# Gathered rows in two permanent buffers, an early signal for one strip, one output tile, and new prologue and epilogue orders, in a residual-chain kernel on one core

## The chip, the core and the metric

The kernel runs on one core of a Trainium2 chip. The core has four computing engines that run their own instruction streams: TensorE (PE in the profile, PEld for its weight loads), VectorE (DVE), ScalarE (ACT) and GpSimd (POOL). SyncE (SP) issues most of the transfers; 16 DMA engines carry them. Streams meet only at semaphores. The metric is the device time of one execution in microseconds (us), as the median of the runs.

## The reference, cut to what matters

A tensor x of 128 entries, 64 rows each, 256 features, passes through four residual layers. Each layer takes its weights or gains from a condition vector of the entry or from class ids of the row:

```python
x = x + einsum('bsd,bde->bse', x, weight(U, V)) + bias     # L0: U = mu @ W_dec + b_dec, rank 30
x = x + clip((x * style) @ weight.T * dcoef + bias)          # L1: modulated product
x = x + (relu(x @ w_down) @ w_up + x)                        # L2: w_down, w_up scaled per entry (dg, ug, ub)
h = ln(ln(x, pw_g[pathway], pw_b[pathway]), cp_g[c], cp_b[c])
t = ln(x, tm_g[c], tm_b[c]);  s = ln(x, ms_g[m], ms_b[m])
cat = concat(w0*h, w1*t, w2*(x+mem), w3*(x+noi), w4*(x+res), w5*s)
x = x + ln(silu(cat @ W1 + b1) @ W2 + b2, g, be)             # L3
```

`pw_g[pathway]` and `pw_b[pathway]` are 512 numbers for each of the 8192 rows, out of a table with 250 rows.

## The kernel before, in words

The 8192 rows are cut into 16 chunks of 512 rows (8 entries). About 70 stages, each a small function of one chunk, carry a chunk through the four layers. A stage is called with its engine and a chunk, waits for its semaphores, and issues its instructions. The order in which an engine runs the stages is written out by hand in three lists for `run_slots`: `begin` (the setup, mixed with the first chunks), `order` (one iteration of the steady loop; a stage with lag 3 works on the chunk three behind the iteration's number; ten iterations, numbers 6 to 15) and `end` (the last chunks). An engine runs its list strictly in order, so a stage that waits holds all stages behind it.

The setup decodes U for all entries (16 groups: `act_turn`/`v_turn`, `pe_dec`, `v_decode`), and makes the per-entry tables: `style` and `dcoef` for L1, `dgdb` and `ugub_scratch` for L2, and the row that L3 adds for each entry (`pe_mo`, `v_mostat`, `g_moroot`, `v_monorm`, `pe_mot`, `pe_row`, `v_rows`, `act_rowwrite`), besides the split weights of L3 (`act_w1scale`, `v_w1sum`, `act_w1high`, `g_w1tlow` and others).

The stages that the argument follows, for a chunk c, in the order of the data:

- `act_u`, `pe_t`, `act_th1`, `act_th2`, `g_tlow`, `pe_x1`, `v_x1add`: layer 0. `pe_t` makes 30 rows t. `act_th1` brings them to SBUF (`t_f`), `act_th2` copies them rounded into three strips of `t_st`, and `g_tlow` overwrites the first strip with what the rounding lost. Each of the two ACT stages adds one to the semaphore `a_th`.
- `g_style`, `pe_l1`, `v_l1mul`, `v_l1min`, `v_x2add`: layer 1.
- `pe_dn`, `v_dnmul`, `v_dnadd`, `act_relu`, `g_wup` (two POOL operations on the tile `ugub`, which `load_up` has filled), `pe_up`, `v_x3sum`: layer 2.
- `pe_x3r`, `v_xstat`, `g_rootx`, `act_x3`, `act_xnorm`, `pe_xht`: the first norm of layer 3 (`xhat`).
- `g_gather`: four indirect DMAs, issued by POOL, that fetch the 512 gathered table rows into `pw_rows`. `g_hmul` multiplies `xhat` with their first half and `g_hadd` adds the second; `v_hstat`, `g_rooth`, `act_hnorm`, `v_hprod`, `pe_hht` follow.
- `pe_w1_x3`, `pe_w1_tm`, `pe_w1_ms`, `pe_w1_h`, `act_silu`, `v_sillow`, `pe_w2`, `act_ysquare`, `g_rooty`, `v_ygain`, `v_ynorm`, `store`: the two products of layer 3 and the output.
- `pe_warm` issues matmuls on a tile of ones, with no use of their result; the table `WARM` says which semaphore each group waits for and how many there are.

There is one `pw_rows`, so `g_gather(c)` waits for `g_hadd(c-1)`. There are two output tiles `y_out`; `v_ynorm(c)` waits until the store of chunk c-2 has landed. All SP transfers, loads and stores, stand in one order: in an iteration ids, shift, x, ub, up, and the store last.

## Time and profile before

| | |
|---|---|
| median of 3 runs | 519.87 us (519.48 to 520.92) |
| the profiled execution, its own time | 522.03 us |
| its span, first to last instruction | 520.2 us |
| PE busy in the span | 486.5 us (94%), 3216 matmuls |
| DVE / ACT / POOL busy | 411.8 / 356.9 / 406.3 us |
| moved by DMA | 61.82 MB |

A span of one engine's busy time near the length of a stretch says that this engine sets the pace there; where it is shorter, the timeline says after each gap in brackets what the engine waited for. The granted clock (PEclk) is a share of TensorE's full 2.4 GHz: 1.00 is 2.4 GHz and 0.50 is 1.2 GHz.

### The profile page before, as it was taken

What the parts mean: (1) busy time and instruction counts of PE and PEld (TensorE: products, weight loads), DVE (VectorE), ACT (ScalarE), POOL (GpSimd) and SP (SyncE); (2) the same over time, 40 slices, a digit from 0 to 9 for tenths busy, and PEclk for the clock granted to TensorE, in tenths of its full rate; (3) what the DMA queues carried; (4) which work ended last, traced back from release to release, by engine and by line L of the source; (5) the groups of instructions that cost most, each with busy time, mean ns of one, the idle gap of its engine ahead of it and who ended that gap; (6) DMA issues with size and microseconds to landing.
All of it is one profiled execution on the core that took longest, in us unless ns stands there. A gap on an engine that the chain in (4) does not pass through costs nothing.

```text
span 520.2 us, 9616 instructions
## 1 busy us (share of the span) xinstructions
PE 486.5 (94%) x3216; PEld 360.9 (69%) x3245; DVE 411.8 (79%) x701; ACT 356.9 (69%) x667; POOL 406.3 (78%) x380
## 2 busy tenths in 40 slices
...
DMA packets 35118, 61.82 MB, mean 119 GB/s; under 512 B 5108, under 2 KB 17542, under 8 KB 34709
## 3 DMA queue, kind: packets, MB, share of 16 engines
...
## 4 chain that ended last, share of the span: by engine, by line
PE 74%; ACT 8%; DVE 7%; issue 5%; POOL 4%; DMA 1%; DVEq 0%; ACTq 0%; POOLq 0%
PE ps_d L966 10%; PE ps_c L916 9%; PE ps_c L918 9%; PE ps_c L917 9%; PE ps_d L980 5%; PE ps_a L994 4%; PE ps_b L916 3%; PE ps_b L917 3%; PE ps_b L918 3%; PE ps_b L1012 3%; PE ps_a L1006 2%; POOL pw_rows L1532 2%; PE ps_a L1012 2%; DMA set_wdec<-in_W_dec 1%; PE ps_b L935 1%
## 5 line engine op out<-in xcount | busy, mean ns | idle before, releaser
L1232 ACT ACTIVATE h<-h,nb_h,rstd_h 128x256 f32<-128x256 f32 x64 | 33.3, 591 | 41.1 <-POOL nb_h L1562 41.1
L966 PE MATMUL ps_d<-xm_t,l_w 128*128 128x512 f32 x128 | 59.6, 609 | 1.6 <-DVE h L1455 0.9
L1532 POOL DMA_INDIRECT pw_rows<-in_pw,gidx x40 | 39.0, 976 | 12.2 <-issue 12.2
L1577 POOL TENSOR_TENSOR h<-xhat,pw_rows 128x1024 f32<-128x1024 f32 x16 | 38.0, 2372 | 6.4 <-ACT xhat L1232 6.4
L966 PEld LDWEIGHTS ps_d<-xm_t,l_w 128*128 128x128 f32 x128 | 23.5, 193 | 26.6 <-issue 24.5
L1598 POOL TENSOR_TENSOR w_up<-w_up,ugub 128x1024 f32<-128x1024 f32 x16 | 39.0, 2436 | 1.3
L1582 POOL TENSOR_TENSOR h<-h,pw_rows 128x1024 f32<-128x1024 f32 x16 | 38.3, 2394 | 1.2
L1596 POOL TENSOR_TENSOR w_up<-up_rep,ugub 128x1024 f32<-128x1024 f32 x16 | 38.1, 2379 | 1.1 <-issue 0.9
L1608 POOL TENSOR_TENSOR x3be<-x,ln_gb 128x1024 f32<-128x1024 f32 x16 | 37.9, 2371 | 0.6 <-DVE y_out L1513 0.6
L916 PE MATMUL ps_b<-w_h,act_t_l 128*128 128x256 f32 x128 | 37.7, 294 | 0.4 <-DVE act_t_l L1477 0.4
L994 PE MATMUL ps_a<-act_dn,w_up 128*128 128x128 f32 x256 | 32.5, 281 | 5.9 <-ACT act_dn L1211 5.3
L994 PEld LDWEIGHTS ps_a<-act_dn,w_up 128*128 128x128 f32 x256 | 31.1, 195 | 9.0 <-issue 7.2
L1343 ACT ACTIVATE y_sq<-ps_b 128x256 bf16<-128x256 f32 x64 | 23.6, 378 | 18.9 <-PE ps_b L918 18.9
L1232 ACT ACTIVATE xhat<-ps_a,nb_x,rstd_x 128x256 f32<-128x256 f32 x64 | 30.9, 563 | 7.9 <-POOL nb_x L1562 7.9
L917 PE MATMUL ps_b<-w_l,act_t_h 128*128 128x256 f32 x128 | 36.1, 282 | 0.0
L918 PE MATMUL ps_b<-w_h,act_t_h 128*128 128x256 f32 x128 | 36.0, 281 | 0.0
L1455 DVE TENSOR_TENSOR h<-ps_d,h 128x1024 f32<-128x1024 f32 x16 | 19.6, 1224 | 18.0 <-ACT h L1232 15.0
L1445 DVE TENSOR_TENSOR ps_d<-ps_d,xh_t 128x1024 f32<-128x1024 f32 x16 | 19.7, 1229 | 17.5 <-PE ps_d L1049 17.5
L1263 ACT ACTIVATE tm_t_h<-ps_a 128x1024 fp32r<-128x1024 f32 x16 | 16.4, 1025 | 25.0 <-DVE ps_a L1440 25.0
L1379 DVE TENSOR_TENSOR ps_d<-ps_d,dcoef 128x1024 f32<-128x1024 f32 x16 | 19.7, 1232 | 15.0 <-PE ps_d L966 13.7
L1532 POOL DMA_INDIRECT pw_rows<-in_pw,pw_idx x24 | 24.1, 1003 | 9.1 <-issue 6.5
L1200 ACT ACTIVATE t_st<-idx_t 30x512 fp32r<-30x512 f32 x48 | 30.0, 625 | 0.5
...
## 6 DMA issues: line engine op xcount, KB each, us to landing
...
pw_rows<-in_pw,gidx POOLq DMA_INDIRECT x40
```

Source lines behind the costliest of these rows:

```text
L916: eng.matmul(out, wl, ah, start=first, stop=False)
L917: eng.matmul(out, wh, al, start=False, stop=False)
L918: return eng.matmul(out, wh, ah, start=False, stop=last)
L966: m = eng.matmul(ps_l1[:, o, :], l1_w[:, k, o * P:(o + 1) * P], xm_t[:, k, :], start=k == 0, stop=k == KB - 1)
L994: m = eng.matmul(ps_up[:, k, j * P:(j + 1) * P], w_up[:, j, k * P:(k + 1) * P], act_dn[:, j, :, :], start=True, stop=True)
L1232: m = eng.activation(out[:, j, :], src[:, j, :], ACT.Identity, bias=nb[k][:, j:j + 1], scale=rstd[k][:, j:j + 1])
L1532: eng.indirect_dma_start(pw_rows[:, j, :], None, t["pw"], bass.IndirectOffsetOnAxis(ap=idx[:, j:j + 1], axis=0)).then_inc(s_pw[c.ring], 16)
L1577: eng.tensor_tensor(h1[:, :, :], xhat[:, :, :], pw_rows[:, :, 0:D], ALU.mult).then_inc(g_h1m, 1)
L1582: eng.tensor_tensor(h1[:, :, :], h1[:, :, :], pw_rows[:, :, D:2 * D], ALU.add).then_inc(g_h1, 1)
L1596: eng.tensor_tensor(w_up[:, :, :], q, ugub[:, :, 0:D], ALU.mult).then_inc(g_upm, 1)
L1598: eng.tensor_tensor(w_up[:, :, :], w_up[:, :, :], ugub[:, :, D:2 * D], ALU.add).then_inc(g_up, 1)
L1608: eng.tensor_tensor(x3be[c.ring][:, :, :], x3[:, :, :], ln_be[:, :].unsqueeze(1).broadcast_to([P, CT, D]), ALU.add).then_inc(g_x3be, 1)
```

## The change

Six edits go together.

1. `pw_rows` becomes two tiles, one for even and one for odd chunks. `g_gather(c)` waits for `g_hadd(c-2)`. Gathers 0 and 1 stand one behind the other near the top of POOL's `begin`, while the decoder runs.
2. `act_th2` signals after its first strip, so `a_th` counts three for a chunk, and `g_tlow` waits for the first strip only. All other waits on `a_th` are renumbered to the same events.
3. To make room, several setup tiles move into tiles that are idle during the setup (`wsq` and `style2` in `w_up`, `dm` and `st_nr` in `x3_t`, `ugub_row` in `dn_v` and `dn`), with waits where the tile is first used (`v_x1add(1)`, `v_dnmul(0)`, `v_x3low(0)`).
4. One `y_out` instead of two: `v_ynorm(c)` waits for the store of chunk c-1. The last two chunks write into `xm_t` and `x1_even` and wait for no store. In SP's loop the store moves ahead of `load_up` and serves the chunk one later (lag 5 for 6).
5. `act_u(0)` is split in two halves, the first of which waits for 8 of the 16 decoder groups.
6. New `begin` and `end` orders on all five engines, and other counts in `WARM`. The loop orders of PE, ACT, DVE and POOL are unchanged.

```diff
-        pw_rows = sb("pw_rows", [P, CT, 2 * D])
+        pw_rows = [sb(f"pw_rows{r}", [P, CT, 2 * D]) for r in range(2)]
...
-        y_out = [late(f"y_out{r}", [P, CT, D]) for r in range(2)]
+        y_out = late("y_out", [P, CT, D])
...
+        y_late = {NCH - 2: rows_in(xm_t), NCH - 1: rows_in(x1_even)}
...
-        WARM = ((z_pool, 1, ps_b, 0, 24), (c_ug, 1, ps_d, 0, 17), (v_dca, 1, ps_a, 0, 8), (v_row, 1, ps_c, 0, 5),
-                (v_cls, 1, ps_c, 1, 2), (v_row, 1, ps_c, 0, 15), (v_ub, 1, ps_b, 1, 6))
+        WARM = ((z_pool, 1, ps_b, 0, 24), (c_ug, 1, ps_d, 0, 11), (v_dca, 1, ps_a, 0, 11), (v_row, 1, ps_c, 0, 8),
+                (v_cls, 1, ps_c, 1, 3), (v_row, 1, ps_c, 0, 3), (v_ub, 1, ps_b, 1, 8))
...
 def act_u
+            if first(c):
+                eng.wait_ge(v_dec, NG // KB)
+                eng.activation(u_ch[0][:, 0], src[:, 0], ACT.Copy)
+                eng.wait_ge(v_dec, NG)
+                eng.activation(u_ch[0][:, 1], src[:, 1], ACT.Copy).then_inc(a_u, 1)
+                return
...
 def act_th2
-            for lo in (0, RP, 2 * RP):
+            eng.activation(t_st[0:RK, :], t_f, ACT.Copy).then_inc(a_th, 1)
+            for lo in (RP, 2 * RP):
...
 def v_ynorm
-            wait(eng, s_store[c.ring], 16 * c.half)
+            if isinstance(c.n, int) and c.n in y_late:
+                wait(eng, p_l1, NCH)
+                wait(eng, v_x3t, NCH - 1)
+            else:
+                wait(eng, s_store[1 - c.ring], 16 * (c.half + c.ring))
...
 def g_gather
-            wait(eng, g_h1, c.n)
+            wait(eng, g_h1, c.n - 1)
+            wait(eng, s_pw[c.ring], 16 * CT * c.half)
...
 def g_tlow
-            wait(eng, a_th, 2 * c.n + 2)
+            wait(eng, a_th, 3 * c.n + 2)
...
 SP
-                      order=[(load_ids, 2), (load_shift, 3), (load_x, 0), (load_ub, 0), (load_up, 0), (store, 6)],
+                      order=[(load_ids, 2), (load_shift, 3), (load_x, 0), (load_ub, 0), (store, 5), (load_up, 0)],
...
 PE begin, from the last decoder group on
-                             (pe_dec, 14), (pe_dec, 15), (pe_ug, 0), (pe_warm, 6), (pe_t, 0), (pe_warm, 1),
-                             (pe_x1, 0), (pe_dc, 0), (pe_t, 1), (pe_hid, 0), (pe_l1, 0), (pe_mo, 0), (pe_x1, 1),
-                             (pe_dn, 0), (pe_t, 2), (pe_warm, 2), (pe_up, 0), (pe_x3r, 0), (pe_l1, 1),
-                             (pe_x1, 2), (pe_mot, 0), (pe_xht, 0), (pe_cls, 0), (pe_dn, 1), (pe_row, 0),
-                             (pe_t, 3), (pe_cp, 0), (pe_up, 1), (pe_warm, 3), (pe_warm, 4), (pe_x3r, 1),
-                             (pe_hht, 0), (pe_l1, 2), (pe_warm, 5), (pe_shift, 0), (pe_tm, 0), (pe_dn, 2),
-                             (pe_w1_x3, 0), (pe_ms, 0)],
+                             (pe_dec, 14), (pe_dec, 15), (pe_ug, 0), (pe_warm, 6), (pe_dc, 0), (pe_t, 0),
+                             (pe_warm, 1), (pe_x1, 0), (pe_hid, 0), (pe_t, 1), (pe_l1, 0), (pe_x1, 1),
+                             (pe_mo, 0), (pe_dn, 0), (pe_warm, 2), (pe_t, 2), (pe_up, 0), (pe_mot, 0),
+                             (pe_x3r, 0), (pe_l1, 1), (pe_x1, 2), (pe_cls, 0), (pe_xht, 0), (pe_dn, 1),
+                             (pe_row, 0), (pe_t, 3), (pe_up, 1), (pe_cp, 0), (pe_warm, 3), (pe_x3r, 1),
+                             (pe_warm, 4), (pe_warm, 5), (pe_l1, 2), (pe_shift, 0), (pe_hht, 0), (pe_w1_x3, 0),
+                             (pe_tm, 0), (pe_dn, 2), (pe_ms, 0)],
...
 DVE begin, behind the first chunk's x1
-                             (v_w2centre, 0), (v_dcrcp, 0), (v_softmax, 0), (v_l1mul, 0), (v_l1min, 0),
-                             (v_x2add, 0), (v_x1add, 1), (v_w1sum, 0), (v_dnmul, 0), (v_dnadd, 0),
-                             (v_mostat, 0), (v_x3sum, 0), (v_xstat, 0), (v_monorm, 0), (v_l1mul, 1),
+                             (v_softmax, 0), (v_dcrcp, 0), (v_w2centre, 0), (v_l1mul, 0), (v_l1min, 0),
+                             (v_x2add, 0), (v_mostat, 0), (v_x1add, 1), (v_dnmul, 0), (v_dnadd, 0),
+                             (v_monorm, 0), (v_x3sum, 0), (v_w1sum, 0), (v_xstat, 0), (v_l1mul, 1),
...
 POOL begin
-                      begin=[(g_ones, 0), (g_init, 0), (g_gather, 0), (g_b2rows, 0), (g_tlow, 0), (g_style, 0),
-                             (g_dcoef, 0), (g_tlow, 1), (g_wup, 0), (g_style, 1), (g_moroot, 0), (g_w1tlow, 0),
-                             (g_tlow, 2), (g_w1xlow, 0), (g_rootx, 0), (g_w2low, 0), (g_w1mlow, 0), (g_hmul, 0),
-                             (g_hadd, 0), (g_wup, 1), (g_rooth, 0), (g_style, 2), (g_gather, 1), (g_res, 0),
-                             (g_rootx, 1), (g_wup, 2), (g_hmul, 1), (g_tlow, 3), (g_hadd, 1), (g_gather, 2),
-                             (g_rooth, 1), (g_style, 3), (g_res, 1), (g_rootx, 2)],
+                      begin=[(g_ones, 0), (g_init, 0), (g_gather, 0), (g_gather, 1), (g_b2rows, 0), (g_tlow, 0),
+                             (g_style, 0), (g_dcoef, 0), (g_tlow, 1), (g_wup, 0), (g_moroot, 0), (g_style, 1),
+                             (g_tlow, 2), (g_rootx, 0), (g_w1tlow, 0), (g_hmul, 0), (g_hadd, 0), (g_wup, 1),
+                             (g_rooth, 0), (g_style, 2), (g_w1xlow, 0), (g_res, 0), (g_rootx, 1), (g_w1mlow, 0),
+                             (g_w2low, 0), (g_wup, 2), (g_hmul, 1), (g_tlow, 3), (g_hadd, 1), (g_res, 1),
+                             (g_rooth, 1), (g_style, 3), (g_gather, 2), (g_rootx, 2)],
...
 POOL end, its first two chunks
-                      end=[(g_wup, 13), (g_hmul, 12), (g_hadd, 12), (g_tlow, 14), (g_rooty, 10), (g_gather, 13),
-                           (g_rooth, 12), (g_res, 12), (g_style, 14), (g_rootx, 13), (g_wup, 14), (g_hmul, 13),
+                      end=[(g_wup, 13), (g_gather, 13), (g_hmul, 12), (g_rooty, 10), (g_hadd, 12), (g_tlow, 14),
+                           (g_res, 12), (g_rooth, 12), (g_style, 14), (g_wup, 14), (g_rootx, 13), (g_hmul, 13),
...
 ACT end, its first stages
-                      end=[(act_hnorm, 12), (act_u, 15), (act_silu, 11), (act_silh, 11), (act_th1, 15),
+                      end=[(act_u, 15), (act_hnorm, 12), (act_silu, 11), (act_th1, 15), (act_silh, 11),
```

## Rows read from the trace of the kernel before

**Rows 1.** The page: its first line and the busy time of TensorE.

```profile
span 520.2 us, 9616 instructions
PE 486.5 (94%) x3216; PEld 360.9 (69%) x3245; DVE 411.8 (79%) x701; ACT 356.9 (69%) x667; POOL 406.3 (78%) x380
```

**Rows 2.** Windows, PE alone: stretch, busy and matmuls, granted clock, DMA share.

```profile
core 0: us, PE busy (x), PEclk, DMA share, GB/s
50.00:100.00 50.00, 40.41 (x263) 0.93 0.36 97
100.00:400.00 300.00, 297.83 (x2024) 1.00 0.41 111
...
455.00:510.00 55.00, 50.42 (x282) 1.00 0.19 58
```

**Rows 3.** Windows again, for the DMA engines and the clock in the setup.

```profile
24.00:46.00 22.00, 18.09 (x146) 1.00 1.01 290
46.00:52.00 6.00, 5.04 (x62) 1.00 0.04 15
...
57.40:64.00 6.60, 5.19 (x20) 0.50 0.29 87
```

**Rows 4.** Timeline of PE, setup: start, length, what, idle time before.

```profile
50.48 1.90 PE L542 MATMUL ps_a<-ones 128*128 128x512 bf16 x8
56.27 2.85 PE L994 MATMUL ps_a<-act_dn,w_up 128*128 128x128 f32 x16 [3.89 <-ACT act_dn L1211]
60.53 1.94 PE L1006 MATMUL ps_a<-ident,x_t 128*128 128x128 f32 x8 [1.41 <-DVE x_t L1419]
...
100.22 1.04 PE L1012 MATMUL ps_a<-ident,xhat 128*128 128x128 f32 x8
```

**Rows 5.** Timeline of POOL, setup.

```profile
22.64 0.95 POOL L1532 DMA_INDIRECT pw_rows<-in_pw,pw_idx  x1 [0.30 <-issue]
...
46.40 2.38 POOL L1596 TENSOR_TENSOR w_up<-up_rep,ugub 128x1024 f32<-128x1024 f32 x1
...
57.63 0.20 POOL L833 TENSOR_SCALAR set_mo_ve<-set_mo_mv 128x3 f32<-128x3 f32 x1 [4.11 <-DVE set_mo_mv L644]
...
83.53 1.12 POOL L1532 DMA_INDIRECT pw_rows<-in_pw,pw_idx  x1 [0.16 <-issue]
...
88.45 2.37 POOL L1608 TENSOR_TENSOR x3be<-x,ln_gb 128x1024 f32<-128x1024 f32 x1
```

**Rows 6.** Timeline of DVE, setup.

```profile
48.86 2.90 DVE L685 TENSOR_TENSOR set_w1x<-set_wdec 128x512 f32<-128x512 f32 x1 [0.39 <-ACT set_wdec L772]
51.80 2.27 DVE L686 TENSOR_TENSOR set_w1x<-set_w1x,set_wdec 128x512 f32<-128x512 f32 x1
...
59.16 1.22 DVE L1419 SCALAR_TENSOR_TENSOR x_t<-x_even,ps_a 128x1024 f32<-128x1024 f32 x1 [1.62 <-PE ps_a L994]
...
64.08 0.38 DVE L1430 BATCH_NORM_AGGREGATE mv_x<-bn_x 128x2 f32<-128x6 f32 x4
...
66.84 0.96 DVE L655 TENSOR_TENSOR set_mo<-ps_c,set_wdec 128x768 f32<-128x768 f32 x1
```

**Rows 7.** DMA queues from 83.5 to 92: packets, MB, share of 16 engines.

```profile
q0 software_dynamic: 320, 1.05, 36.2%
```

**Rows 8.** Timeline of PE, epilogue.

```profile
413.82 0.65 PE L935 MATMUL ps_b<-x_t,u_ch 128*30 128x64 f32 x32 [0.87 <-ACT u_ch L1181]
...
463.66 0.50 PE L916 MATMUL ps_c<-ms_t_h,w_l 128*128 128x512 f32 x1 [0.92 <-DVE ms_t_l L1464]
...
474.59 0.39 PE L1092 MATMUL ps_c<-onehot,shift 128*128 128x512 bf16 x1 [0.87 <-DVE act_t_l L1483]
...
491.08 0.39 PE L1026 MATMUL ps_a<-onehot,gain_tab 24*128 24x512 bf16 x2 [1.08 <-ACT xh_t L1253]
```

**Rows 9.** Timelines of DVE and SP around an output, end of the loop.

```profile
406.22 1.66 DVE L1513 SCALAR_TENSOR_TENSOR y_out<-ps_b,rstd_y,x3be 128x256 f32<-128x256 f32 x4
...
435.44 1.66 DVE L1513 SCALAR_TENSOR_TENSOR y_out<-ps_b,rstd_y,x3be 128x256 f32<-128x256 f32 x4
```

More of the change, by code:

```diff
@@ L402, in split_in_place, with y_tile @@
             link(eng.tensor_copy(p3, src))
+        def y_tile(c):
+            return y_late[c.n] if isinstance(c.n, int) and c.n in y_late else y_out
         v_link = chain(nc.vector, v_chain)
@@ L1368, in v_x1add @@
             if isinstance(c.n, int) and c.n == 1:
-                eng.wait_ge(m_dc, 1)
+                eng.wait_ge(m_tail, 1)
                 eng.wait_ge(m_st, 1)
                 eng.wait_ge(m_ug, 1)
+                eng.wait_ge(m_hid, 1)
+                eng.wait_ge(d_ub, 48)
+                eng.wait_ge(v_pick, 1)
             eng.tensor_tensor(x1_t[c.ring][:, :, :], ps_x1[:, :, :], x_t[c.ring][:, :, :], ALU.add).then_inc(v_x1, 1)
@@ L1466, in low @@
             return stage
-        v_x3low = low(x3_t_l, x3_t, x3_t_h, a_x3h, v_x3l, (m_tail, 1), (m_st, 1), (m_ug, 1), (m_hid, 1), (d_ub, 48))
+        v_x3low = low(x3_t_l, x3_t, x3_t_h, a_x3h, v_x3l, (v_mo, 2))
         v_tmlow = low(tm_t_l, ps_tm, tm_t_h, a_tmh, v_tml, (m_row, 1), (d_row, 16))
@@ L1692, in _ @@
-                             (act_th1, 4), (act_x3, 2), (act_xnorm, 2), (act_hh, 1), (act_th2, 4), (act_tmh, 1),
-                             (act_x3h, 2), (act_relu, 3), (act_ysquare, 0), (act_msh, 1), (act_xht, 2),
-                             (act_gidx, 3), (act_onehot, 2)],
+                             (act_turn, 13), (act_turn, 15), (act_dg, 0), (act_vhigh, 0), (act_style, 0),
+                             (act_ug, 0), (act_exp, 0), (act_u, 0), (act_u, 1), (act_th1, 0), (act_th2, 0),
+                             (act_sqrt, 0), (act_u, 2), (act_hid, 0), (act_th1, 1), (act_th2, 1),
@@ L1734, in _ @@
                            (v_l1min, 13), (v_x2add, 13), (v_hlow, 11), (v_tmprod, 11), (v_dnmul, 13),
-                           (v_dnadd, 13), (v_tmlow, 11), (v_msprod, 11), (v_hstat, 12), (v_mslow, 11),
-                           (v_ygain, 10), (v_ynorm, 10), (v_x3low, 12), (v_x1add, 14), (v_x3sum, 13),
+                           (v_dnadd, 13), (v_tmlow, 11), (v_msprod, 11), (v_ygain, 10), (v_mslow, 11),
+                           (v_ynorm, 10), (v_hstat, 12), (v_x3low, 12), (v_x1add, 14), (v_x3sum, 13),
@@ L1737, in _ @@
                            (v_hprod, 12), (v_xstat, 13), (v_sillow, 11), (v_l1mul, 14), (v_l1min, 14),
                            (v_x2add, 14), (v_hlow, 12), (v_tmprod, 12), (v_dnmul, 14), (v_dnadd, 14),
-                           (v_tmlow, 12), (v_msprod, 12), (v_hstat, 13), (v_mslow, 12), (v_ygain, 11),
-                           (v_x3low, 13), (v_ynorm, 11), (v_x3sum, 14), (v_x1add, 15), (v_hprod, 13),
+                           (v_tmlow, 12), (v_hstat, 13), (v_msprod, 12), (v_ygain, 11), (v_x3low, 13),
@@ L1741, in _ @@
+                           (v_mslow, 12), (v_ynorm, 11), (v_x3sum, 14), (v_hprod, 13), (v_x1add, 15),
                            (v_xstat, 14), (v_sillow, 12), (v_l1mul, 15), (v_l1min, 15), (v_x2add, 15),
-                           (v_hlow, 13), (v_tmprod, 13), (v_dnmul, 15), (v_tmlow, 13), (v_dnadd, 15),
-                           (v_x3low, 14), (v_msprod, 13), (v_hstat, 14), (v_ygain, 12), (v_mslow, 13),
-                           (v_x3sum, 15), (v_ynorm, 12), (v_hprod, 14), (v_sil0, 13), (v_xstat, 15),
@@ L1745, in _ @@
-                           (v_msprod, 14), (v_sil1, 13), (v_hlow, 14), (v_tmprod, 14), (v_mslow, 14),
-                           (v_tmlow, 14), (v_hstat, 15), (v_ygain, 13), (v_x3low, 15), (v_ynorm, 13),
-                           (v_sil0, 14), (v_sil1, 14), (v_tmprod, 15), (v_hprod, 15), (v_tmlow, 15),
-                           (v_msprod, 15), (v_hlow, 15), (v_mslow, 15), (v_ygain, 14), (v_ynorm, 14),
+                           (v_hlow, 13), (v_tmprod, 13), (v_x3low, 14), (v_dnmul, 15), (v_dnadd, 15),
```

136 lines of the change are left out of this document (73 added, 63 removed).

## The prediction

> **What bounds the kernel now.** I began with the page's totals: TensorE is busy 94% of the span [rows 1]. The windows of PE say where the rest is [rows 2]. From 100 to 400 us it is busy 297.83 of 300, so in the loop nothing but PE's own work counts. Two stretches are loose: 50 to 100 (40.41 of 50, and part of that is `pe_warm`) and 455 to 510 (50.42 of 55, 4.6 idle). The change leaves PE's useful instructions and all loop orders but SP's alone, so it can act only through how early the loop starts and how tightly the epilogue packs. Next I read PE's timeline for what ends its gaps, then the engines named there, and last the DMA windows.
>
> In the setup PE runs eight warm matmuls at 50.48, then waits 3.89 us for `act_relu(0)` and starts `pe_up(0)` at 56.27; `pe_x3r(0)` waits 1.41 more [rows 4]. DVE shows why: between `v_x1add(1)` and `v_dnmul(0)` stands `v_w1sum`, 2.90 and 2.27 us [rows 6], where an operation with twice the elements takes 1.22 in the same rows. During it POOL is in `g_wup(0)`, from 46.40 [rows 5]. Behind the gap the granted clock is 0.50, the 1.2 GHz level, from 57.4 to 64 [rows 3]; eight transposes that take 1.04 at full clock (at 100.22) took 1.94 there [rows 4]. The loop's first `pe_xht` is at 100.22 [rows 4], my mark for the end of the setup.
>
> The second fact is the DMA engines: share 1.01 from 24 to 46, then 0.04 [rows 3]. Until 46 us they are full, and what comes last out of that backlog is `ugub` for chunk 0. `g_wup(0)` starts at 46.40 [rows 5], which is when the backlog ends.
>
> **The change part by part, setup.** The sum is made against the profiled execution (span 520.2, own time 522.03). The median of the runs is 519.87, so 2.2 us come off at the end.
>
> *Gather 1 moved.* Its POOL time is 83.53 to 88.45, 4.9 us [rows 5]. There it sits in front of `g_res(0)`, `g_rootx(1)`, `g_wup(2)` and `g_hmul(1)`, thus of the path to the loop. Behind gather 0 (last piece at 22.64, [rows 5]) it takes 4.9 us of a stretch in which POOL has little to do: `g_b2rows` slips by 4.9, and `g_tlow(0)`, with ACT now running `act_exp` and `act_u(1)` first, by about 1.5. What that delays is `pe_x1(0)`; `pe_dc`, the exponential and a `u` that used to lie behind it now lie ahead, so I find `v_x2add(0)` within 0.3 us of before. Of the 4.9 saved, `g_w1xlow`, `g_w1mlow` and `g_w2low`, which move behind, take 3.8 back (three operations of 512 columns; half of the 2.37 of 1024 in [rows 5] plus overhead, 1.25 each). Net gain: 1.1.
>
> *Gather 1 as traffic.* A gather took 36.2% of 8.5 us of all 16 engines, 3.1 us [rows 7]. At 24 to 29 us it is put in front of a full backlog, so that ends at 49.4, not 46.3, if nothing overlaps; 46.3 if the gather hides wholly. From DMA: Bandwidth & Descriptors, in the Trainium skill, section on SWDGE, HWDGE and iDMA: each engine goes round-robin over its queues. Hence GpSimd's queue would get its share at once, at the cost of SP's. With that page's 436 GB/s the estimate would be 2.4 us of delay instead of 3.1.
>
> *The new order in front of `pe_up(0)`.* `v_w1sum` moves behind `v_x3sum(0)`, `v_mostat` in front of `v_dnmul(0)`. Now `v_dnmul`, `v_dnadd` and `v_mostat` fill the 3.6 us from the end of `v_w1sum` at 54.07 [rows 6] to `g_moroot` at 57.63 [rows 5]; I give `v_mostat`, the longest, 2.4. The dn path ends at 56.3 - 5.1 + 2.4 = 53.6. The other leg is `g_wup(0)`: 4.8 us from the landing. Landing at 49.4 ends it at 54.2, and `g_moroot` (1.1) follows at 55.3. `v_monorm` now precedes `v_x3sum(0)` and waits for it; it takes 3.4 (64.4 to 67.8, [rows 6]). So `v_x3sum(0)` starts at 58.7 against 59.16, `v_w1sum` with POOL idle costs 1.3 (twice half of 1.22), `v_xstat(0)` 2.0, and mv_x is ready at 63.3, against 64.46 [rows 6]: 1.2 earlier. With the landing hidden, `g_wup(0)` starts as soon as POOL is free, by my walk at 44.3, and ends at 49; `v_monorm` then waits for `v_dnadd(0)` only, starts at 52.8, and mv_x is ready at 60.8: 3.7 earlier. Where between? The 0.50 clock may return, since PE still has two gaps of some 2 us here; that costs 0.9 on `pe_x3r(0)`, the difference in [rows 4]. I take the DMA delay as full, for the rows say full, and the clock as half likely.
>
> The setup then gives 1.2 + 1.1 = 2.3, up to 4.8 with the landing hidden, 1.4 with the slow clock. The row write of the setup gains a little because gather 1 no longer runs beside it. I take 2.5.
>
> *Early strip, `act_u` halves.* `act_th2` is three equal copies, so `g_tlow` may start two copies (1.3 us) earlier. In the loop PE never waits for it. In the setup it is inside the sum above. At nothing beyond that; if POOL were late it could give 1.3 once.
>
> *Moved tiles and their waits.* All are long past when asked: `v_x1add(1)` waits for `m_hid`, `d_ub`, `v_pick`, some 10 us old. Zero. If `m_hid` were late, `v_x1add(1)`, `v_mostat`'s successors and all of chunk 0's dn would queue behind it.
>
> **Loop.** `v_ynorm` comes at 406.22 and 435.44, one period apart, 27 to 29 us [rows 9]. The store now issues right behind it, since SP's waits in front of it (shift, x, ub) end earlier in the iteration; half a megabyte takes a few us at the 111 GB/s mean of [rows 2] (4.7). So the one tile has over 20 us of slack. `load_up` now stands behind the store, and what is queued behind it are the next ids, shift and x; but its own wait for `g_wup` ends later in the iteration than `v_ynorm` does. Zero. Bound: a late store would cost its lateness in each of ten iterations.
>
> **Epilogue.** Idle that names a cause: 0.87 for `u_ch(15)`, 0.92 for `ms_t_l`, 0.87 for `act_t_l`, 1.08 for `xh_t` [rows 8], and 4.6 in all from 455 to 510 [rows 2]. `act_u(15)` goes first on ACT, which removes the first. But gather 13 goes in front of `g_hmul(12)`: `g_hadd(12)` is 6 us later, `g_tlow(14)` too, and `pe_x1(14)` moves ahead of `pe_up(13)`. I walked these chunks: PE waits 0.4 for `ms_t_l(11)`, 0.5 for `g_tlow(14)` and 0.5 for `xhat(13)`. Net -0.5. In the next iteration `g_res(13)`, `g_style(15)` and gather 14 come out ahead, +0.6. In the last two, PE waits at most 1 us in five places where it waited 4.1. Sum: -0.5 + 0.6 + 3.1 = 3.2; my walk has no semaphore latency, so 2.7. Bounds 0.5 and 4. The tail behind the last product keeps its stages.
>
> **Sum.** 2.5 + 0 + 2.7 = 5.2. Span 515.0, profiled 516.8, median 514.7.
>
> **Rivals.**
> A. *Gather 1 hides in the backlog.* For it: the share counts overlap (1.01 is not a hard wall). Against: nothing idle from 24 to 46. Setup 4.8, sum 7.5: 512.4. Chance 0.17.
> B. *The backlog and the clock eat the setup's gain.* `ugub(0)` lands at 50 and PE stays at 0.50 for 7 us again. Setup about 0, epilogue 2.7: 517.2. Chance 0.20.
> C. *Nothing: the loop's start takes it back.* PE's idle in the loop is 2.2 of 300 [rows 2], so an earlier start can hardly be lost there; the epilogue would have to be pure shuffling, held by POOL and DVE. 519.5. Chance 0.07.
> D. *Slower: `ugub(0)` decides.* From the landing on the path is one for one: `g_wup`, `g_moroot`, `v_monorm`, `v_x3sum`. A landing at 49.4 leaves the setup 2.3 ahead, one at 51.7 nothing, and from 54.4 on (51.7 and the epilogue's 2.7) the kernel is slower. For it, `g_wup(0)` already starts as the backlog ends, and broadcast loads and the gather share engines. Against, that takes 8 us of delay where [rows 7] show 3.1. At 56: setup -4.3, epilogue 2.7, 521.5. Chance 0.06.
> A side risk within all: `v_w1sum` shows that a DVE operation with two SBUF operands waits while POOL computes, 2.90 for 0.6 of work [rows 5, 6]. `v_x3low(14)` now meets `g_wup(15)`: up to 1.6, inside my epilogue bound. (SBUF — State Buffer, section "SBUF: two separate sides", in the Trainium skill calls it an exclusive lock held for a whole instruction; the trace agrees.)
>
> **How the numbers follow.** Forecast 0.50, A 0.17, B 0.20, C 0.07, D 0.06. A measurement here tells 0.3% (1.6 us) from no change. Forecast and A are faster; of B, three in twenty fall within 0.3%; C is same, D slower: faster 0.84, same 0.10, slower 0.06. Eight in ten: from 511.4 (A with a full epilogue) to 518.4 (B with an epilogue of 1.5). The forecast's own range is 513 to 516.5.
>
> **What would show it.** PE's first loop `pe_xht` near 97.7 (A: 95.4; B: 100; D: past 103). POOL's `w_up` start near 49.4 with idle in front of it. DMA share near 1 until 49. No 0.50 clock, or a shorter one. `v_w1sum` at 1.3 us. PE idle from 455 on down from 4.6 to about 1.5, with new small gaps near 400 to 420 from `g_tlow(14)`. `v_ynorm` never waiting for a store. A loop period that differs, or idle there, would make me wrong at the root.

## The result and the profile after

Six runs of the changed kernel gave a median of 524.00 us (521.74 to 525.21); the kernel before had 521.24 beside it. The ratio is 1.0057, 95% interval 1.0036 to 1.0078: slower by 0.6%, where I had forecast 514.7 and a range up to 518.4. Measured again with a later group (`c0_after` below) the same kernel had 531.76 against 522.25, ratio 1.0153 (1.0108 to 1.0198). So the loss is real and not always of one size.

The page's first lines, and the windows of PE that answer to [rows 1, 2]:

```profile
span 523.4 us, 9602 instructions
PE 485.3 (93%) x3207; PEld 361.2 (69%) x3236; DVE 417.8 (80%) x701; ACT 355.9 (68%) x667; POOL 406.7 (78%) x380
```

```profile
50.00:100.00 50.00, 40.71 (x279) 0.97 0.35 84
100.00:400.00 300.00, 294.78 (x1990) 0.99 0.43 112
455.00:510.00 55.00, 51.29 (x290) 1.00 0.13 39
```

PE is busy for as long as before; the span is 3.2 longer. The middle row is the surprise: 294.78 in the stretch where [rows 2] had 297.83, so 3 us of new idle time lie in the loop, which no loop order of PE, ACT, DVE or POOL explains. DVE is busy 6 us longer with the same 701 instructions: something made them last longer.

PE's timeline, the rows that answer to [rows 4, 8]:

```profile
54.45 2.02 PE L1001 MATMUL ps_a<-act_dn,w_up 128*128 128x128 f32 x16 [0.93 <-ACT act_dn L1223]
59.46 1.06 PE L1013 MATMUL ps_a<-ident,x_t 128*128 128x128 f32 x8 [0.28 <-DVE x_t L1435]
98.02 1.06 PE L1019 MATMUL ps_a<-ident,xhat 128*128 128x128 f32 x8 [0.57 <-DVE tm_t_l L1480]
106.46 0.80 PE L923 MATMUL ps_c<-ms_t_h,w_l 128*128 128x512 f32 x1 [2.82 <-DVE ms_t_l L1480]
130.14 1.10 PE L1019 MATMUL ps_a<-ident,xhat 128*128 128x128 f32 x8
...
403.11 1.04 PE L1019 MATMUL ps_a<-ident,xhat 128*128 128x128 f32 x8
410.93 0.71 PE L960 MATMUL ps_b<-t_st,v_st 96*128 96x512 f32 x2 [0.87 <-POOL t_st L1569]
419.25 3.67 PE L973 MATMUL ps_d<-xm_t,l_w 128*128 128x512 f32 x8 [0.94 <-DVE h L1471]
432.87 1.04 PE L1019 MATMUL ps_a<-ident,xhat 128*128 128x128 f32 x8
```

The setup did what was forecast in this trace: the first loop `pe_xht` is at 98.02 (97.7 forecast, 100.22 before). Then the first iteration, number 6, takes 32.12 us to the next mark, where the kernel before took 27.44. The lead of 2.2 becomes a lag of 2.5 there, and it stays: just behind the loop the mark is 403.11 against 400.66.

DVE and POOL around that gap (both timelines of the changed kernel; the second number is the length):

```profile
98.82 6.46 DVE L1480 TENSOR_TENSOR x_t_l<-x_t,x_t_h 128x1024 fp32r<-128x1024 f32 x1
105.20 1.21 DVE L1480 TENSOR_TENSOR ms_t_l<-ps_d,ms_t_h 128x1024 fp32r<-128x1024 f32 x1
```

```profile
98.25 1.28 POOL L1569 TENSOR_TENSOR t_st<-idx_t,t_st 30x512 fp32r<-30x512 f32 x1 [0.47 <-ACT t_st L1210]
99.50 2.39 POOL L1603 TENSOR_TENSOR h<-h,pw_rows 128x1024 f32<-128x1024 f32 x1
101.85 2.34 POOL L1629 TENSOR_TENSOR x3be<-x,ln_gb 128x1024 f32<-128x1024 f32 x1
108.40 0.20 POOL L1575 TENSOR_TENSOR nm_h<-mv_h,mone 128x4 f32<-128x4 f32 x1 [4.21 <-DVE mv_h L1446]
```

This is nearly all of iteration 6's loss of 4.7 us. `v_x3low(1)` subtracts one SBUF tile from another; alone it takes 1.22. It starts at 98.82, while POOL computes, and ends at 105.28, 1.1 us after POOL's third operation in a row ends (104.19). `v_mslow(0)`, now behind it in DVE's order, is 4 us late, PE waits 2.82 for it, and the granted clock falls: 0.79 of full speed as the mean of 104 to 112. `pe_w1_ms(0)` behind the wait starts 8.4 us after the mark, where it started 5.6 after it before, and takes 4.4 us for 2.9: 2.8 from the wait and 1.5 from the clock. POOL then waits 4.21 for what DVE has not done. In the kernel before, gather 2 stood between `g_hadd(1)` and `g_res(1)`, and `v_mslow(0)` ahead of `v_x3low(1)`.

### The profile page after: what moved, and what is told of

Its sections match the earlier page's. It is cut to its first block, busy times and chain, and to the rows that moved or that the text cites. A ratio compares the mean times of both kernels' runs of the same rounds, so it can differ in the third digit from the quotient of the medians.

```text
span 523.4 us, 9602 instructions
## 1 busy us (share of the span) xinstructions
PE 485.3 (93%) x3207; PEld 361.2 (69%) x3236; DVE 417.8 (80%) x701; ACT 355.9 (68%) x667; POOL 406.7 (78%) x380
## 4 chain that ended last, share of the span: by engine, by line
PE 65%; POOL 11%; DVE 9%; DMA 6%; issue 4%; ACT 3%; SPq 0%; DVEq 0%; POOLq 0%; ACTq 0%
PE ps_d L973 8%; PE ps_c L923 8%; PE ps_c L925 8%; PE ps_c L924 8%; PE ps_d L987 4%; PE ps_a L1001 4%; PE ps_b L923 3%; POOL pw_rows L1553 3%; PE ps_b L924 3%; PE ps_b L925 2%; DMA ugub<-ugub_scratch 2%; PE ps_b L1019 2%; PE ps_a L1013 2%; PE ps_a L1019 2%; DVE x_t_l L1480 2%
## 5 line engine op out<-in xcount | busy, mean ns | idle before, releaser
L1598 POOL TENSOR_TENSOR h<-xhat,pw_rows 128x1024 f32<-128x1024 f32 x16 | 40.0, 2500 | 5.5 <-ACT xhat L1244 5.5
L1244 ACT ACTIVATE xhat<-ps_a,nb_x,rstd_x 128x256 f32<-128x256 f32 x64 | 30.9, 564 | 9.3 <-POOL nb_x L1583 9.3
L923 PE MATMUL ps_c<-ms_t_h,w_l 128*128 128x512 f32 x64 | 27.2, 425 | 2.9 <-DVE ms_t_l L1480 2.8
```

Source lines behind the costliest of these rows:

```text
L923: eng.matmul(out, wl, ah, start=first, stop=False)
L1244: m = eng.activation(out[:, j, :], src[:, j, :], ACT.Identity, bias=nb[k][:, j:j + 1], scale=rstd[k][:, j:j + 1])
L1598: eng.tensor_tensor(h1[:, :, :], xhat[:, :, :], pw_rows[c.ring][:, :, 0:D], ALU.mult).then_inc(g_h1m, 1)
```

## The experiments

The median of the kernel before was 521.3 to 522.3 beside the groups below. "Mark 6" is the first loop `pe_xht`, "mark 17" is `pe_xht(12)`, the second one of PE's end list; up to it the marks keep the loop's distance of 27.2 in both kernels. The groups ran on different chips (first and second on one, third, fourth and fifth on others), so between groups the ratios compare better than the medians.

**First group: is it the lock, and where?**

`e1_both`: the changed kernel, with two spots of its begin orders as they were. `e2_pool` has only the POOL part of the edit, `e3_dve` only the DVE part.

```diff
 POOL begin
-(g_hadd, 1), (g_res, 1), (g_rooth, 1), (g_style, 3), (g_gather, 2), (g_rootx, 2)
+(g_hadd, 1), (g_gather, 2), (g_rooth, 1), (g_style, 3), (g_res, 1), (g_rootx, 2)
 DVE begin
-(v_msprod, 0), (v_x3low, 1), (v_mslow, 0), (v_hstat, 1)
+(v_msprod, 0), (v_mslow, 0), (v_x3low, 1), (v_hstat, 1)
```

> The changed kernel with two spots of its begin orders as they were before: on POOL gather 2 behind g_hadd(1), then g_rooth, g_style, g_res; on DVE v_mslow(0) ahead of v_x3low(1). Theory T (lock): iteration 6 loses 4.7 us because v_x3low(1), two SBUF operands, waits out three POOL operations that stand back to back (6.46 us for 1.22) and ms_t_l is queued behind it. Then v_x3low(1) takes about 1.2, the first loop pe_xht stays at 98.0, the second comes at 125.5 instead of 130.14, and the time falls by 4 to 4.7 to 519.3 to 520. Rival L (the loop's start takes any lead back, by a path that these orders do not touch): second pe_xht at 128 or later, 522 to 524. Rival E (the epilogue lost it): under 1 us of change.

> Only the POOL half of the repair: g_gather(2) behind g_hadd(1), g_res(1) last but one. Theory T: v_x3low(1) starts at 98.8, waits for g_hadd(1) to end at 101.9 and lasts about 4.2 in place of 6.46; ms_t_l ends at 104.2, PE idles 0.6 instead of 2.82 and its clock stays at 1.00. Time down by 3.5 to 4.7: 519.5 to 520.5. Rival L: no change, 523 to 524.5.

> Only the DVE half: v_mslow(0) ahead of v_x3low(1), POOL as in the changed kernel. Theory T: ms_t_l at 101.5 (its PSUM operand does not wait for POOL), PE has no idle time there; v_x3low(1) still lasts 2 to 3 us until POOL falls idle at 104.2, but only v_hstat(1) stands behind it. Time down by 3 to 4.7: 519.5 to 521. If instead gather 2, now at 115 and not at 104, is what hurts, e3 gains nothing and e2 gains all.

Measured: 526.39 (ratio 1.0093, 1.0063 to 1.0123), 526.31 (1.0062, 1.0029 to 1.0095) and 526.53 (1.0108, 1.0074 to 1.0142). By the times beside the 524.00 of the changed kernel my theory was dead: I had expected 519.5. The trace of `e1_both` says otherwise, PE first, then DVE:

```profile
102.34 1.06 PE L1019 MATMUL ps_a<-ident,xhat 128*128 128x128 f32 x8 [0.58 <-DVE tm_t_l L1480]
130.37 1.04 PE L1019 MATMUL ps_a<-ident,xhat 128*128 128x128 f32 x8
```

```profile
106.92 1.22 DVE L1480 TENSOR_TENSOR x_t_l<-x_t,x_t_h 128x1024 fp32r<-128x1024 f32 x1
```

Iteration 6 is repaired: 28.03 us, `v_x3low(1)` lasts 1.22, PE does not wait for `ms_t_l`. With the DVE part alone `v_x3low(1)` still lasts 2.69, as expected, PE does not wait for `ms_t_l`, and the iteration takes 28.49; with the POOL part alone it lasts 4.47, and the iteration takes 28.92. But mark 6 itself is at 102.34, 102.55 and 102.61 in the three, 4.3 to 4.6 us later than in the changed kernel's trace, and nothing of the edit lies ahead of it. A second loss was there that the first trace did not show.

`e4_oldend`: the changed kernel, with the end orders of PE, ACT, DVE and POOL as before.

> The changed kernel with the end orders of PE, ACT, DVE and POOL as before (SP's stays). From the second-last marks I read that the new epilogue is worth nothing or costs up to 1 us (403.1 to the end: 120.3 us, before 119.5 from 400.7). So 523 to 524. If the new epilogue had given the 2.7 of the prediction, with the loss all in iteration 6, this run would be at 526.7.

Measured 531.53 (1.0204, 1.0170 to 1.0238). The control below puts the changed kernel itself at 531.76 on that chip, so the old end changed nothing that the medians can tell. The marks tell more: from mark 17 to the end of the span it took 119.5 us (408.20 to 527.7), as in the kernel before (400.66 to 520.2), and the changed kernel 120.3. The new end orders cost about 1 us; they give nothing.

**Second group: the setup.** `c0_after` is the changed kernel again. The other edits, on POOL (in `c1_g1old` and `c2_nogather` `act_gidx(3)`, which waits for gather 1, also goes back to the end of ACT's begin; both have the two repairs):

```diff
 c1_g1old
-(g_gather, 0), (g_gather, 1), (g_b2rows, 0)
+(g_gather, 0), (g_b2rows, 0) ... (g_style, 2), (g_gather, 1)
 c2_nogather
-(g_gather, 0), (g_gather, 1), (g_b2rows, 0)
+(g_b2rows, 0), (g_gather, 0) ... (g_tlow, 2), (g_gather, 1)
```

`e5_oldbegin` takes the whole begin orders of PE, ACT, DVE and POOL and `WARM` from the kernel before.

> The changed kernel unchanged, on the chip of this group, as the base of the other three. New theory G (the gathers beside the decoder): the issues of 8 indirect DMAs on POOL from 17.7 to 28 hold up the signals between PE, DVE and ACT in the decoder; in the four traces with both gathers there the last v_decode came at 30.3, 30.2, 30.5 and 28.8 where the first trace of the changed kernel has 26.3, and pe_x1(0) at 39.4 to 42.2 against 35.3. Then this run shows a late decoder in most executions: 524 to 526, last v_decode 28 to 30.5.

> The changed kernel with both repairs of iteration 6 and with gather 1 back at its old place on POOL, behind g_style(2) (act_gidx(3), which waits for it, back at the end of ACT's begin). Theory G: the decoder meets 4 issues instead of 8, its last v_decode is at 25 to 27, and ugub for chunk 0 lands at 45 to 46.5. Gather 1's 4.9 us on POOL are then in the setup again: first loop pe_xht 98 to 101, iteration 6 takes 27.5 to 28, sum 519 to 521.5, 5 us below the repaired kernel with both gathers early (526.4). Rival R (the setup of the new orders is late by itself, whatever the gathers): last v_decode at 29 to 30 again and 525 or more.

> As the last, but gather 0 stands behind g_b2rows(0), where POOL waited 4 us for t_st, and gather 1 behind g_tlow(2), where it waited 4.7 us for mv_x. Theory G: almost no issue falls into the decoder, last v_decode at 24.5 to 25.5 (PE's own time), first loop pe_xht 95.5 to 98, iteration 6 27.5 to 28: 516 to 519, below both kernels. Rival R: no gain over c1_g1old beyond 1 us.

> The changed kernel with the begin orders of PE, ACT, DVE and POOL and the WARM counts of the kernel before (gather 1 late, v_mslow ahead of v_x3low); two gather tiles, early strip, one output tile, later stores, SP's order and the new end orders stay. If the loss is all in the begin orders and the end is worth nothing (-0.8 to +0.5 us), this is the kernel before within 1 us: 521 to 523. If one output tile, the early strip or the moved tiles cost time, 524 or more; if the new end gives the 2.7 forecast, 519.

Measured: 531.76, then 524.22 (1.0044, 1.0022 to 1.0065), 521.81 (0.9990, 0.9975 to 1.0005) and 521.06 (0.9978, 0.9957 to 0.9998). The control has both losses at once: mark 6 at 102.86 and 308.15 us from there to mark 17, where the repaired kernel takes 300.05. Against this control the three repairs of iteration 6 gained 5.2 to 5.5 us, as my theory of the lock had said (4 to 4.7); either half of the edit is enough. Taking gather 1's 4.9 us out of POOL's early part and putting them back on the old path made the kernel faster by 2.2 us. `c2_nogather` is faster by 2.4 more, but it moves two things: gather 0 off the decoder, and gather 1 from behind `g_style(2)` into a wait of POOL behind `g_tlow(2)`. `d1_b_gather0` below moves gather 0 alone and gains nothing. Both versions stayed 3 us above what I had expected of them. In the control the last steps of the decoder on DVE are these:

```profile
24.28 0.69 DVE L607 TENSOR_TENSOR u_all<-ps_a,set_bdec 128x512 f32<-128x512 f32 x1 [2.26 <-issue]
27.84 0.69 DVE L607 TENSOR_TENSOR u_all<-ps_a,set_bdec 128x512 f32<-128x512 f32 x1 [2.86 <-remote]
29.31 0.69 DVE L607 TENSOR_TENSOR u_all<-ps_c,set_bdec 128x512 f32<-128x512 f32 x1 [0.78 <-remote]
30.24 0.42 DVE L607 TENSOR_TENSOR u_all<-ps_c,set_bdec 128x256 f32<-128x256 f32 x1
```

**Third group: issues or bytes, and a version that is faster.** `d1_b_gather0` moves gather 0 behind `g_b2rows(0)` in the kernel before. `d2_oldorders` is the changed code with all begin and end orders and `WARM` old (SP's new). `d3_moved` is `d2_oldorders` with gather 0 behind `g_b2rows(0)` and gather 1 ahead of `g_moroot(0)`. `d4_narrow` is `c1_g1old` with a stage behind gather 0:

```diff
+        def g_narrow(eng, c):
+            settle(eng, s_idle)
+            for j in range(CT):
+                eng.indirect_dma_start(pw_rows[1][:, j, 0:16], None, t["pw"].rearrange("a (b c) -> (a b) c", c=16),
+                                       bass.IndirectOffsetOnAxis(ap=pw_idx[:, CT + j:CT + j + 1], axis=0)).then_inc(s_pw[1], 16)
```

> The kernel before with one stage moved: gather 0 behind g_b2rows(0) on POOL. Theory G (gathers beside the decoder hold it up): in the kernel before the third-last v_decode waited 0.65 us and the last ended at 25.9; with the four issues now from about 24.7 on, the last v_decode ends near 25.3 or earlier, worth up to 1 us: 521 to 522. Rival R (the stall has another cause): the same waits as before, 522.

> The changed kernel with begin and end orders of PE, ACT, DVE and POOL, and the WARM counts, as before; what stays is the code: two gather tiles, the early strip, act_u in halves, moved tiles, one output tile, SP's order. From first loop mark 12 to the end the old end orders took 119.5 us in two traces and the new ones 120.3 to 121.0 in five. So 1.2 us below the run with only the begin orders old (521.06): 519.5 to 520.3. If the new end orders were a gain, it is slower than that run.

> The last kernel with the two gathers placed by what the traces show: gather 0 behind g_b2rows(0), gather 1 ahead of g_moroot(0), where POOL waited 4.1 us, and so off the path behind g_style(2). Theory G and the prediction's first term (4.9 us of POOL ahead of the loop): first loop pe_xht 1.5 to 4 us earlier, 516 to 518.5. Rival L (the start of the loop takes it back, as the order there is tuned to gather 1's place): 519.5 to 521.

> The repaired kernel with gather 1 late (524.2 measured) plus four narrow indirect DMAs behind gather 0, which bring 16 columns of 512 into the tile that gather 1 overwrites later: the issues of two gathers beside the decoder, with 3% of the second one's bytes. If the issues on POOL hold up the decoder, its last v_decode is at 28.5 to 30.5 as with both gathers, and the time 527 to 529. If the gather's traffic on the DMA engines does it, the last v_decode is at 25.5 to 26 and the time 524 to 525.

Measured: 521.92 (0.9994, 0.9966 to 1.0022), 519.52 (0.9956, 0.9932 to 0.9980), 523.92 (1.0040, 1.0016 to 1.0063) and 528.43 (1.0127, 1.0080 to 1.0174). `d2_oldorders` beats both kernels; by its ratio it is also 0.2% below `e5_oldbegin`, from which only the old end orders part it. `d3_moved` refutes my placement: POOL was free at 54.84, 1.7 us before the input of `g_moroot(0)` was there (56.55), the four issues (55.00 to 59.78) put it off to 59.85, and mark 6 is at 102.43 against 100.04. `d4_narrow` is a verdict for the issues by its median, 4.2 us above `c1_g1old`, but its trace has the last `v_decode` at 25.9. That trace is of an execution of 525.53 us, the second fastest of six (524.25 to 531.14), so it does not show what the slower four did.

**Fourth group.** `f1_b_narrow` puts the same narrow stage into the kernel before (target `w_up`); `f2_c2oldend` is `c2_nogather` with the old end orders; `f3_b_strip` is the kernel before with the early strip and `act_u(0)` in halves, parts 2 and 5 of the change, and no order touched; `f4_b_lock` puts the two spots of the first diff, in the reverse direction, into the kernel before.

> The kernel before plus four narrow indirect DMAs right behind gather 0 (16 columns of 512 each, into w_up, which is idle there and is written over later): the early issues of the change alone, with 3% of the bytes. Theory G (issues on POOL hold up the decoder): last v_decode ends at 28.5 to 30.7 instead of 25.9 in most executions, 525 to 527. Rival B (the bytes do it, or other parts of the new begin orders): last v_decode by 26.5, g_tlow(0) at most 1 us later, 522 to 523.

> The version with both repairs of iteration 6 and the gathers off the decoder (521.81 measured, setup mark 98.61) with the old end orders on PE, ACT, DVE and POOL. The old end took 119.5 us from mark 12 on, the new one 120.7 there: 520 to 520.8. If the new begin orders are worth their 1.4 us at the setup mark against the version with all orders old (100.04, 519.52 measured), this one comes below it: 518.5 to 519.5.

> The kernel before with the early signal for the first strip and act_u(0) in two halves, nothing else. The version with all orders old was 0.44% below the kernel before. If these two parts of the code give that, by an earlier g_tlow(0) and pe_x1(0), this run is at 519.5 to 520.5; if the second gather tile, the store order or one output tile do it, it is at 521.5 to 522.5. The prediction's value for it was nothing to 1.3.

> The kernel before with only the two spots of the begin orders that the repair put back, put in: g_res(1) behind g_hadd(1) and gather 2 behind g_style(3) on POOL, v_x3low(1) ahead of v_mslow(0) on DVE. Theory T (lock): v_x3low(1) lasts 5 us or more, ms_t_l follows late, PE idles 2.5 to 3 us, iteration 6 takes 31 to 32.5 instead of 27.44: 526 to 529. Rival: the new orders before it are needed for the loss; then 522 to 523.

Measured: 525.30 (1.0100, 1.0061 to 1.0139), 520.54 (0.9984, 0.9966 to 1.0002), 519.53 (0.9957, 0.9938 to 0.9976) and 529.16 (1.0129, 1.0094 to 1.0165). `f4_b_lock` makes the first loss in the kernel before, with an unchanged setup (mark 6 at 100.24, [rows 4] has 100.22). DVE, PE and ACT of its trace:

```profile
101.58 5.08 DVE L1464 TENSOR_TENSOR x_t_l<-x_t,x_t_h 128x1024 fp32r<-128x1024 f32 x1
106.58 1.21 DVE L1464 TENSOR_TENSOR ms_t_l<-ps_d,ms_t_h 128x1024 fp32r<-128x1024 f32 x1
```

```profile
107.85 0.50 PE L916 MATMUL ps_c<-ms_t_h,w_l 128*128 128x512 f32 x1 [1.77 <-DVE ms_t_l L1464]
122.37 1.09 PE L1012 MATMUL ps_b<-ident,h 128*128 128x128 f32 x8 [2.65 <-ACT idx_t L1189]
```

```profile
121.21 1.11 ACT L1189 ACTIVATE idx_t<-ps_b 30x128 f32<-30x128 f32 x4 [4.27 <-remote]
```

Its mark 7 is at 134.10: iteration 6 takes 33.86 for 27.44. Three stages in another place cost 6.4 us in the trace and 7.2 in the median. But only the first 2.0 us are the wait for `v_x3low(1)`: `pe_w1_ms(0)` starts at 107.85 for 105.81. The other 4.4 stand behind a second wait. ACT's `act_th1(4)` starts at 121.21, though `pe_t(4)`, its input, ends at 116.1 and `g_tlow(3)`, the other stage it waits for, at 100.9; `pe_hht(1)` waits 2.65 for it, and the granted clock is 0.66 in 122 to 127, which costs 1.6 more. While ACT waits, POOL issues gather 2 (115.41 to 120.21). The same wait of `act_th1(4)` beside gather 2 is in `c0_after` (3.79) and `e4_oldend` (3.88), not in the first trace of the changed kernel and not in the three repaired ones. It comes with the late iteration 6, but its cause is not shown. `f3_b_strip` shows where the changed code gains; its POOL and PE:

```profile
30.97 1.26 POOL L1553 TENSOR_TENSOR t_st<-idx_t,t_st 30x512 fp32r<-30x512 f32 x1 [2.45 <-ACT t_st L1203]
...
43.01 1.26 POOL L1553 TENSOR_TENSOR t_st<-idx_t,t_st 30x512 fp32r<-30x512 f32 x1 [1.13 <-ACT t_st L1203]
```

```profile
32.87 0.70 PE L953 MATMUL ps_b<-t_st,v_st 96*128 96x512 f32 x2
97.56 1.04 PE L1012 MATMUL ps_a<-ident,xhat 128*128 128x128 f32 x8
```

`g_tlow(0)` started at 32.29 in the kernel before and `g_tlow(1)` at 45.10; the second is 2.1 earlier. `g_wup(0)` behind it is only 0.8 earlier (45.63, it now waits 1.36 for `ugub`), but the first operation of `v_w1sum` now takes 0.69 in place of 2.90 (the second 2.73 for 2.27), and mv_x is ready at 61.79, 2.7 earlier.

**Fifth group.** `h1_narrow2` has the orders of `e1_both`, but gathers 0 and 1 fetch 16 columns of 512, so chunks 0 and 1 leave out most of their table product. `h2_w1sum` is `f3_b_strip` with `v_w1sum` moved as in the change:

```diff
 h2_w1sum, DVE:  -(v_x1add, 1), (v_w1sum, 0), (v_dnmul, 0)    +(v_x3sum, 0), (v_w1sum, 0), (v_xstat, 0)
           ACT:  -(act_relu, 0), (act_w1high, 0)              +(act_th2, 2), (act_w1high, 0)
           POOL: -(g_moroot, 0), (g_w1tlow, 0)                +(g_rootx, 0), (g_w1tlow, 0)
                 -(g_tlow, 2), (g_w1xlow, 0)                  +(g_style, 2), (g_w1xlow, 0)
```

> The changed kernel with both repairs of iteration 6 and both gathers early, where gathers 0 and 1 bring only 16 columns of 512 (the other columns of the two tiles are zeros, so chunks 0 and 1 leave out most of that product): eight issues beside the decoder in the same order, with 3% of their bytes. The same with all bytes: 526.4, last v_decode ended at 30.6 to 30.9 in three traces. If the issues on POOL hold up the decoder: the same, 525 to 527. If the bytes do: last v_decode by 26.5, first loop pe_xht 3 to 4 us earlier (98 to 99.5), 522 to 523.5. Two memsets on DVE are added at 2 to 8 us, where it idles 4 us.

> The kernel before with the early strip and act_u(0) in halves (519.53 measured, first loop pe_xht at 97.56) and v_w1sum moved behind v_x3sum(0), with act_w1high, g_w1tlow and g_w1xlow moved behind it as in the change. The prediction's second term: v_w1sum (2.90 and 2.27 us beside g_wup(0)) falls off the path to pe_up(0) and mv_x is ready earlier, 1.2 us. If so: mark near 96.4, 518.3 to 518.8. If v_x3sum(0) waits for something else by then, no gain: 519 to 520.

Measured: 519.29 (0.9969, 0.9945 to 0.9993) and 520.48 (0.9985, 0.9961 to 1.0009). `h1_narrow2` has the same eight issues as `e1_both` and is 7 us below it (on another chip; by the ratios it is 1.2%, 6.5 us): eight issues with hardly any bytes hold up nothing. That is not yet "the bytes do it". `d4_narrow` and `f1_b_narrow` add four issues with 3% of a gather's bytes behind a full gather, and their medians rise by 4.2 and 3.4 us; four of the six executions of the one (527.91 to 531.14) and two of the six of the other (529.26 and 530.09) stand 3 to 6 us above the rest. Some 1 to 2 us of each is POOL's own time for the four issues (`g_tlow(0)` at 33.91 for 32.62, and at 34.36 for 32.29). What is shown is that a full gather has to be there; whether the issues beside them or the second gather's bytes do the rest is not separated. DMA queues from 24 to 28 us (packets, MB, share of 16 engines), the control first, then `h1_narrow2`:

```profile
q0 software_dynamic: 343, 1.14, 83.6%
q1 hardware_dynamic: 115, 0.20, 13.9%
```

```profile
q1 hardware_dynamic: 639, 0.83, 63.5%
q0 software_dynamic: 66, 0.02, 3.1%
```

and the last `v_decode` of `h1_narrow2`:

```profile
25.22 0.42 DVE L607 TENSOR_TENSOR u_all<-ps_c,set_bdec 128x256 f32<-128x256 f32 x1
```

The decoder over all traces (end of the last `v_decode` from DVE's timelines, mark 6 from PE's), one execution of each kernel:

| gathers beside the decoder | last `v_decode` ends | mark 6 |
|---|---|---|
| two, full: changed kernel; `c0_after`; `e1_both`, `e2_pool`, `e3_dve`; `e4_oldend` | 26.7; 30.7; 30.7, 30.6, 30.9; 29.2 | 98.0; 102.9; 102.3, 102.6, 102.6; 99.9 |
| one, full: before; `c1_g1old`; `e5_oldbegin`; `d2_oldorders`; `f3_b_strip`; `f4_b_lock`; `h2_w1sum` | 25.9; 26.2; 25.6; 27.0; 25.8; 25.4; 25.8 | 100.2; 99.7; 97.3; 100.0; 97.6; 100.2; 100.3 |
| one full and one narrow: `d4_narrow`; `f1_b_narrow` | 25.9; 25.3 | 99.8; 102.4 |
| two narrow: `h1_narrow2` | 25.6 | 97.1 |
| none: `c2_nogather`; `d1_b_gather0`; `d3_moved`; `f2_c2oldend` | 25.7; 24.9; 24.8; 25.3 | 98.6; 99.9; 102.4; 96.4 |

Narrow issues are not free either: in `f1_b_narrow` they push `g_b2rows(0)` and with it `g_tlow(0)` from 32.29 to 34.36, on the path to `pe_x1(0)`. That, not the decoder, is its mark of 102.4, in the fastest of its six executions.

## Why the prediction was wrong, by its own steps

**The loop, put at zero: the step that failed.** The first trace adds up: the setup gives 2.2, iteration 6 takes 4.7, the end takes 0.8, together the 3.2 by which the span is longer. I wrote that an earlier start "can hardly be lost there", and searched the loop's orders, which are unchanged. But iteration 6 of PE runs beside the last stages of the begin lists of DVE and POOL, and these are not. The mechanism was in my hands as the side risk: [rows 5, 6] show a two-SBUF operation of DVE waiting for POOL, and I priced it once, at `v_x3low(14)`, up to 1.6. I did not ask for every such operation what POOL does at that time in the new order. Asked of `v_x3low(1)`, the new list answers: three POOL operations of 1.3, 2.4 and 2.3 us with no issue between them. Price: 4.7 in the first trace, of which 2.8 is the wait for the lock and 1.5 the clock that fell behind it. In `c0_after` the stretch to mark 17 is 8.1 longer than in `e1_both`, and `f4_b_lock` lost 6.4; there the lock's own wait is 2.8 and 2.0, and the late `act_th1(4)` with the clock behind it, which no order of mine explains, is a large part of the rest. That the loss begins with these three stages is shown, since any half of the repair takes it away; that all of it is the lock is not.

**Gather 1 as traffic: right place, wrong victim.** I charged it to `ugub` for chunk 0: landing 49.4 forecast, and POOL's `w_up` started at 48.65 in the first trace. What I left out is the decoder, which was running at that very time. With both gathers full it ended 3 to 5 us late in five of six traces, and the control's queue rows show the hardware queue, which carries SP's transfers, down to 14% of engine time (40% in the first trace of the changed kernel). The sixth trace is that of the first measurement, so this loss is no part of its 3.2 us; it makes the 531.76 of the control. I had put rival D, slower through a late `ugub(0)`, at 0.06; slower was right, but through the decoder and the lock. By medians, from the repaired kernel on, 526.39 becomes 524.22 without gather 1 beside the decoder, 521.81 with neither there and gather 1 in a better place, 519.29 (another chip) with both there but narrow. What exactly waited is open: in the control's trace the records of PE's last groups end at 24.3 while DVE's steps wait to 29.3, and the profile names only "issue" and "remote". Nor does it take two gathers or a full backlog: ACT waits 3.72 and 3.14 us beside gather 0 alone in `d2_oldorders` and `e5_oldbegin` (to 24.22 and 23.32), and the waits of `act_th1(4)` above stand beside gather 2 at a DMA share of 0.43 to 0.46. All of them run beside the four issues of a gather on POOL and end within 1 us of the last one. No run separated the candidates.

**Setup, +2.5.** In the first trace it was 2.2, and most rows were met: `v_w1sum` 0.68 and 0.69 us (1.3 forecast), mv_x at 62.5 (63.3), clock 1.00 in 57.4 to 64, PE's gap ahead of `pe_up(0)` 0.93. But the runs give the credit to other terms, so that the 2.2 is in part luck. The early strip, which I valued at nothing to 1.3, is worth 2.4 us with `act_u(0)` in halves and nothing else (`f3_b_strip`). The move of `v_w1sum`, which I valued at 1.2, gives nothing on top of it (`h2_w1sum`: ratio 0.9985 against 0.9957): mv_x was ready 0.24 earlier although `ugub(0)` landed 3.7 later, but `g_w1tlow(0)`, 2.4 us of POOL work that moves with it, came between `g_rootx(0)` and `g_hmul(0)`, which started at 68.08 instead of 66.61. And a gather's 4.9 us on POOL is only free where POOL really idles: not ahead of `g_moroot(0)`.

**One output tile, later stores, moved tiles: zero, right.** `d2_oldorders` has all of them and is as fast as `f3_b_strip`, which has none (ratios 0.9956 and 0.9957); the loop period is 27.2 us in both kernels.

**Epilogue, +2.7: wrong in sign, about -1.** Mark 17 to 18 takes 29.76 in the changed kernel and 28.22 before, a loss of 1.5; here I had forecast a loss of 0.5. `g_tlow(14)` behind the moved gather 13 costs 0.87, where I had 0.5. The 0.94 for `h` is the lock again, at `v_x3low(12)` in the end list (DVE, then POOL):

```profile
411.44 2.75 DVE L1480 TENSOR_TENSOR x_t_l<-x_t,x_t_h 128x1024 fp32r<-128x1024 f32 x1
```

```profile
410.75 2.35 POOL L1629 TENSOR_TENSOR x3be<-x,ln_gb 128x1024 f32<-128x1024 f32 x1
413.07 1.18 POOL L1575 TENSOR_TENSOR nm_h<-mv_h,mone 128x4 f32<-128x4 f32 x1
```

`g_res(12)`, now ahead of `g_rooth(12)`, holds `v_x3low(12)` until 413.1; then that operation holds POOL's `nm_h`, 1.18 for its usual 0.20, and `h` comes late. In the kernel before `v_x3low(12)` took 1.22. The named `v_x3low(14)` took 2.97, but it had taken 2.78 in the kernel before already, so this side risk was worth 0.2 and not up to 1.6:

```profile
455.60 2.78 DVE L1464 TENSOR_TENSOR x_t_l<-x_t,x_t_h 128x1024 fp32r<-128x1024 f32 x1
```

Mark 18 to 19 lost another 0.7 (28.06 for 27.36), where I had forecast a gain of 0.6. The last chunks did gain: from the mark at 460.93 to the end 62.5 us, before 64.0 from 456.24, 1.5 where I had forecast 3.1.

One sum of the prediction is also off in itself: A with a full epilogue is 4.8 + 4 = 8.8 below 519.87, 511.1 and not 511.4.

**The balance of the later groups**, by medians: 531.8 for the changed kernel, 526.4 with iteration 6 repaired, 521.8 with the gathers off the decoder too, 520.5 with the old end as well (the last step, in another group, is smaller by the ratios: 0.9990 to 0.9984). What is left is no better than `f3_b_strip`, 519.5: eleven lines of code in the kernel before.
